# Three dense layers of a transformer stack: norm statistics a turn ahead, second norm on ACT, first norm on POOL in two layers, another order of stages, gate softmax once a layer

## The reference

```
x = x + 0.5 * ffn0(norm(x))      # s = norm @ Win + bin; g = sum_h relu(s*W1+b1)*W2 + b2 (64 channels of 16); g @ Wout + bout
x = x + attention(norm(x))       # 16 heads of 8, 4 kv heads, rotary, causal
x = x + 0.5 * ffn0(norm(x))
x = x + 0.5 * experts(norm(x))   # softmax gate over 8 experts, each takes its top 128 of a sequence's 512 tokens, gelu MLP
x = x + scan(norm(x))            # t = norm @ (sum of U*V + toP); lam = sigmoid(sigmoid(norm @ F) @ W_lam)
                                 # s_t = lam*s_(t-1) + (t @ B); h = (t + s @ C) @ fromP
x = x + 0.5 * experts(norm(x))
```

## Time and profile before

| what | value |
|---|---|
| median of three runs | 1877.16 us (1871.71 to 1878.62) |
| the profiled execution | 1875.22 us, span 1873.2 us |
| mean granted clock of PE | 0.915 |
| busy share: PE, PEld, DVE, ACT, POOL | 84%, 59%, 73%, 58%, 41% |

### The profile page before, as it was taken

The page is one execution under the profiler, slowest core; times in us unless marked ns, Lnnn a source line. Parts: engine busy times, 40 slices in busy tenths (PEclk is TensorE's granted clock), DMA queues, the critical chain, the costliest instruction groups (busy, mean ns, idle before and its releaser), DMA issues. The chain is left out here.

```text
span 1873.2 us, 39185 instructions
## 1 busy us (share of the span) xinstructions
PE 1581.5 (84%) x11698; PEld 1107.9 (59%) x11698; DVE 1360.9 (73%) x3422; ACT 1089.0 (58%) x2225; POOL 760.4 (41%) x1170
## 2 busy tenths in 40 slices
PE   4878749999999999998699529999977751999998
PEld 1444424555555555554355329999964531999997
DVE  4898746777777777774388668777768976777776
ACT  2444313666666666666466427787755531877876
POOL 1565542333333333333233256665401212666540
PEclk9989856999999999999899759999988875999999
DMA  5111231111111111110011301111000110121110
GB/s 135 31 38 50 59 105 36 43 43 42 41 41 41 44 39 42 40 35 2 1 34 33 110 19 39 38 34 29 25 1 23 34 34 12 39 60 46 43 48 23
DMA packets 72819, 76.39 MB, mean 41 GB/s; under 512 B 13040, under 2 KB 61488, under 8 KB 72752
## 3 DMA queue, kind: packets, MB, share of 16 engines
q1 hardware_dynamic: 64560, 58.77, 10.9%
q0 software_dynamic: 8192, 16.79, 3.4%
HBM read 51.40 MB, written 24.12 MB: 40 GB/s over the span
## 5 line engine op out<-in xcount | busy, mean ns | idle before, releaser
L951 DVE TENSOR_REDUCE at_negmax<-at_s_ps 128x2 f32<-128x1024 f32 (+3 forms) x384 | 394.5, 1045 | 174.9 <-PE at_s_ps L741 170.4
L862 ACT ACTIVATE at_p<-at_x_ps 128x512 f32<-128x512 f32 x640 | 353.5, 591 | 224.1 <-PE at_x_ps L751 221.3
L918 POOL TENSOR_SCALAR_AFFINE_SELECT at_p<-at_p 128x256 f32<-128x256 f32 (+1 forms) x448 | 190.7, 438 | 354.9 <-ACT at_p L862 354.9
L1175 POOL DMA_INDIRECT e_x_in<-xn,e_row_c x256 | 258.5, 1010 | 145.7 <-POOL e_row_c L1171 103.5
L739 PE MATMUL at_s_ps<-at_kr,at_qr 72*128 72x512 bf16 (+3 forms) x1024 | 253.0, 312 | 20.6 <-DMA at_kr<-k_parts 18.2
L751 PE MATMUL at_x_ps<-at_qr,at_kr 74*128 74x512 bf16 (+3 forms) x1024 | 236.4, 306 | 23.0 <-ACT at_p L862 12.9
L1296 DVE TENSOR_TENSOR e_hid_lo<-e_hid,e_hid_hi 128x512 fp32r<-128x512 f32 x256 | 177.2, 693 | 85.3 <-ACT e_hid_hi L1260 85.3
L741 PE MATMUL at_s_ps<-maskb,identb 128*128 128x128 bf16 x1024 | 202.1, 225 | 0.0
L1259 ACT ACTIVATE e_hid<-e_h_ps 128x512 f32<-128x512 f32 x256 | 155.0, 605 | 39.4 <-PE e_h_ps L1201 38.9
L766 PE MATMUL at_o_ps<-at_p,at_va 128*32 128x512 f32 (+3 forms) x2048 | 157.0, 449 | 1.6 <-POOL at_p L918 1.6
L1201 PE MATMUL e_h_ps<-e_x_hi,w_hi 128*128 128x256 f32 x512 | 156.0, 305 | 0.1
(11 more groups left out here) (184 smaller groups left out, 3515.2 us busy)
## 6 DMA issues: line engine op xcount, KB each, us to landing
at_qr<-q_parts SPq DMA_DIRECT2D x192, 96.0 KB
k_parts<-m_kparts SPq DMA_DIRECT2D x48, 96.0 KB
at_kr<-k_parts SPq DMA_DIRECT2D x64, 72.0 KB
xres<-in_x_dram SPq DMA_DIRECT2D x8, 512.0 KB, 7.3
xn<-m_n_xhat SPq DMA_DIRECT2D x16, 256.0 KB, 2.3
e_x_in<-xn,e_row_c POOLq DMA_INDIRECT x256, 2.5
xn<-sc_n_xhat SPq DMA_DIRECT2D x16, 256.0 KB, 2.3
out_dram<-xres SPq DMA_DIRECT2D x16, 256.0 KB, 2.3
```

What stands on the lines that cost most here:

```text
L862: a.activation(p_sb[g % 2][:, i, :], x_ps[i % 2][:], ACT.Exp, scale=SCALE).then_inc(x_read, 1)
L918: sel = gp.affine_select(out=part, in_=part, compare_op=ALU.is_ge, fill=0.0, base=0, pattern=[[0, n] for n in part.shape[1:-1]] + [[1, P]] ...
L951: v.tensor_reduce(negmax[u][:, h0:h0 + len(heads), c], s_ps[k % 2][:, 0:len(heads) * pitch].rearrange("p (j w) -> p j w", w=pitch)[:, :, 0:w],
L1175: nc.gpsimd.indirect_dma_start(out=x_in[k][u][:], out_offset=None, in_=xn_dram, in_offset=bass.IndirectOffsetOnAxis(ap=row_c[k][:, u:u + 1 ...
```

## The change

A fourth stage, `ahead`, is put before the head: in each turn DVE makes the first norm's statistics of the next turn (`moments`), and the norm is applied there too, by ACT in the qkv layer and by POOL in the gate and scan layers (`gpsimd_all`). The second norm's statistics are made by DVE in the middle stage, right after the residual is added; ACT applies them (`apply`, an Identity with the root as scale and a shift as bias, which POOL computes), in the mlp layers in the same turn as the statistics, in the scan layer a turn later. For the shift DVE also negates the means (`less`). DVE applies no norm any more.

In the mlp layers DVE's turn is now: statistics ahead, output addition and second statistics of the middle, then (qkv) rotations with hidden channels of the head, or (gate) hidden channels of the head. In the gate layer DVE makes 5 of the 8 channels instead of 3; its scores are made a turn later and its banks of PSUM are shared in another way. POOL's turn begins with the bias addition. The gate's softmax is made once at the end of a layer over all 16 sequences, where the scores of each turn are copied to `probs` (`keep`). In the scan layer `ts` has two buffers. All engines of the scan layer but SP, and the gate layer's POOL, run the turns unrolled (`unrolled`) and not in a loop.

In the scan layer the orders are: PE transposes of the head, products of the middle (L1382, L1383), projection of the head, scores of tail - 1, output of the middle, second transposes of the tail; ACT copies of the head, sigmoid of the middle, second norm of the tail, t and sigmoid of the head, second copies of the tail; POOL root and shift of the tail, then root and application for `ahead`; DVE scans of the middle, statistics ahead, `keep`, output addition and second statistics of the middle. In qkv, PE keeps the order of before.
 `moments`, `statistics` and `aggregate` hold the same instructions as `Norm.moments` before, and `root` the same power as L180. In the diff the lines that begin with "#" only say where what follows stands.

```diff
-HV = {"qkv": 5, "gate": 3}
+HV = {"qkv": 5, "gate": 5}
...
+    def widen(self, dve, i):
...
+        self.nc.vector.tensor_scalar(self.less[:], self.mv[:, :, 0], -1.0, None, ALU.mult)
+        self.nc.vector.tensor_scalar(self.vare[:], self.mv[:, :, 1], EPS, None, ALU.add).then_inc(self.var_done, 1)
...
+    def gpsimd(self, pool, i):
+        self.root(pool, i)
+        self.nc.gpsimd.tensor_tensor(self.shift[:], self.less[:], self.rstd[:], ALU.mult).then_inc(self.shift_done, 1)
...
+    def gpsimd_all(self, pool, i, xhat_used):
+        self.root(pool, i)
+        after(pool, xhat_used, i * W)
...
-                s = self.nc.vector.tensor_scalar(
+                s = self.nc.gpsimd.tensor_scalar(
                     self.xhat[b][:, c * D:(c + 1) * D], self.xres[:, i * W + b, c * D:(c + 1) * D],
                     self.mv[:, j, 0:1], self.rstd[:, j:j + 1], ALU.subtract, ALU.mult)
...
+    def apply(self, act, i):
+        act.wait_ge(self.shift_done, i + 1)
...
+                s = self.nc.scalar.activation(
+                    self.xhat[b][:, c * D:(c + 1) * D], self.xres[:, i * W + b, c * D:(c + 1) * D],
+                    ACT.Identity, bias=self.shift[:, j:j + 1], scale=self.rstd[:, j:j + 1])
...
+def unrolled(turn):
+    at = lambda n: n if 0 <= n < TURNS else None
+    for n in range(TURNS + 3):
+        turn(at(n), at(n - 1), at(n - 2), at(n - 3))
...
 # mlp_layer, PE, gate
+                def turn_gate(ahead, head, middle, tail):
+                    if middle is not None:
+                        channels(middle)
+                    if head is not None:
+                        turn_first(head)
+                    if middle is not None:
+                        output(middle, tail)
+                    if head is not None:
+                        project_in(head)
+                    if tail is not None and not is_first(tail):
+                        score(tail - 1)
+                    if tail is not None:
+                        if middle is not None:
+                            pe.wait_ge(x_added, middle * W + W)
+                        turn_second(tail)
...
 # mlp_layer, ACT, behind the head's channels
+                        split(tail, EARLY[:W])
+                    if not qkv and tail is not None:
+                        copy_second(tail)
+                    if middle is not None:
...
+                        norm2.apply(act, middle)
+                    if qkv and ahead is not None:
+                        norm1.apply(act, ahead)
+                    if qkv and tail is not None:
+                        split(tail, EARLY[W:])
...
 # mlp_layer, POOL, behind the bias addition
+                    if qkv and tail is not None and not is_first(tail):
+                        split(tail - 1, LATE)
+                    if ahead is not None:
+                        if qkv:
+                            norm1.gpsimd(pool, ahead)
+                        else:
+                            norm1.gpsimd_all(pool, ahead, xt_full)
+                    if middle is not None:
+                        norm2.gpsimd(pool, middle)
...
 # mlp_layer, DVE
+                def turn(ahead, head, middle, tail):
+                    if ahead is not None:
...
+                        moments(dve, norm1, ahead)
                     if middle is not None:
...
+                        dve.wait_ge(x_added, middle * W + W)
+                        moments(dve, norm2, middle)
+                    for x in range(NT if qkv else W):
+                        if qkv and tail is not None:
+                            rope(tail, x)
+                        if head is not None and x < W:
+                            hidden(head, x)
...
+                    if not qkv and tail is not None and not is_first(tail):
+                        gate.keep(dve, tail - 1)
...
+                    gate.keep(dve, TURNS - 1)
+                    gate.softmax(dve)
```

More of the change, by code:

```diff
@@ new lines, in project_in, with score, turn_qkv @@
+                def project_in(head):
+                    for b in range(W):
+                        pe.wait_ge(xt_read, head * W + b + 1)
+                        pe.matmul(s_ps[b][:], h["win2"][:], xhat_t[b][:], start=True, stop=True).then_inc(s_full, 1)
+                def score(tail):
+                    pe.wait_ge(xt2_read, tail * W + W)
+                    for b in range(W):
+                        gate.tensor(pe, tail, b, xhat2_t[b])
+                def turn_qkv(ahead, head, middle, tail):
@@ L436, in turn @@
                     if tail is not None:
-                        if qkv:
-                            queries(tail, 1)
-                            keys(tail)
-                            values(tail)
-                        else:
-                            for b in range(W):
-                                gate.tensor(pe, tail, b, xhat2_t[b])
-                pipeline(pe, turn)
+                        queries(tail, 1)
+                        keys(tail)
+                        values(tail)
@@ L447, in _ @@
+                pipeline(pe, turn_qkv if qkv else turn_gate)
+                if not qkv:
+                    score(TURNS - 1)
             @block.scalar
@@ L461, in split @@
                             a.activation(r["parts"][:, 1, :], r["b"][:], ACT.Copy).then_inc(p2_done, 1)
-                def turn(head, middle, tail):
-                    if not qkv and tail is not None and not is_first(tail):
-                        gate.scalar(act, tail - 1)
+                def turn(ahead, head, middle, tail):
                     if middle is not None:
@@ L1374, in _, with turn @@
             def _(pe):
-                def turn(head, middle, tail):
+                def turn(ahead, head, middle, tail):
+                    if head is not None:
+                        for b in range(W):
+                            pe.wait_ge(norm1.xhat_done, head * W + b + 1)
+                            if tail is not None and not is_first(tail):
+                                pe.wait_ge(xt2_read, tail * W - W + b + 1)
+                            transpose_chunks(pe, xt_ps[b], norm1.xhat[b], h["ident"]).then_inc(xt_full, 1)
                     if middle is not None:
@@ L1414, in _, with turn @@
                 a = nc.scalar
-                def turn(head, middle, tail):
-                    if tail is not None and not is_first(tail):
-                        gate.scalar(act, tail - 1)
+                def turn(ahead, head, middle, tail):
+                    if head is not None:
+                        for b in range(W):
+                            act.wait_ge(xt_full, head * W + b + 1)
+                            a.activation(xhat_t[b][:], xt_ps[b][:], ACT.Copy).then_inc(xt_read, 1)
                     if middle is not None:
@@ L1451, in _, with turn @@
                 v = nc.vector
-                def turn(head, middle, tail):
-                    if tail is not None:
-                        dve.wait_ge(x_added, tail * W + W)
-                        norm2.moments(dve, tail)
-                        if not is_first(tail):
-                            gate.less_max(dve, tail - 1)
-                    if head is not None:
-                        norm1.moments(dve, head)
-                    if tail is not None:
-                        for b in range(W):
-                            after(dve, xn_out[b], tail * 16)
-                        norm2.apply(dve, tail)
+                def turn(ahead, head, middle, tail):
                     if middle is not None:
```

286 lines of the change are left out of this document (136 added, 150 removed).

## The result

| | before | after |
|---|---|---|
| median of four runs, us | 1875.68 (1871.71 to 1878.62) | 1885.85 (1882.14 to 1887.94) |
| span of the profiled run, us | 1873.2 | 1880.1 |
| mean granted clock | 0.915 | 0.915 |

The account below looks back on a forecast made before the run. DVE was taken to bound qkv and scan, while PE in gate had about 1 us idle a turn. 1875.2 - 26 (qkv) + 15 (gate) - 15 (scan) = 1849.2, about 1850 on the median's footing; range 1832 to 1864.

Parts of the forecast that it names:

- qkv, -26: qkv layer: 26 us shorter, from five turns won 20, start lost 3, end won 10, 1 off; range -38 to -10.
- gate, +15: Gate layer: 15 us longer, 12 from seven turns, 1.5 at the start, 1.5 in the tail.
- the collision: Gate layer: POOL's bias adds, 2.5 us, stretch DVE's hidden channels 5 to 8, adding 1.7 us a turn.
- The ring without collision at 16.5: Gate turn: sum read, output, adds, second moments, DVE's hidden channels, channel sums; 16.5 us, equal to before.
- scan, -15: Scan layer: 122 us against 137.1, a turn 12.1 for 15.4; bounds -22 and -8.
- with pointers I take 0.35, so 2.8 us a norm: POOL's norm: 8 tensor_scalar of 128x128 at 0.35 us each; bounds 0.2 and 1.65 each.
- a ring that took its PE work at warm durations: Scan turn: scans, moments ahead, root, POOL's norm, transposes, lambda product, sigmoid, next scan; 12.1 us a turn.
- about 15 ... as before: Scan layer start: about 15 us after the layer's first instruction, unchanged from before.
- The tail of the scan layer, 25: Scan layer after the last scan: 25 us for output, moments, norm, cold scores and softmax 4.3.
- D: Rival: POOL's tensor_scalar priced like its power, 1.65 us each; 1924, spread over 1860 to 1924; chance 0.14.
- B: Rival: no collision in the gate layer, gate +3, rest as forecast, 1838 (1828 with dense PE in qkv); chance 0.16.
- C: Rival: ACT's queue takes DVE's place in qkv, turn stays at 27, gate and scan as forecast, 1875; chance 0.10.

## Why the prediction was wrong

- **qkv, -26: right, also by its terms.** -28.3 in the profile of after, 24.0 to 27.4 in the twelve others. The five turns win 21.9 us (forecast 20), the start loses 3.8 (3), the end wins 10.2 (10). The turn is 23.5 for the forecast 23.3; ACT's Identity lasts 0.48 one by one, but eight take 3.19 us (forecast 3.2), PE's clock 0.88 before and 1.00 after. DVE also waits there for ACT's application before it may aggregate, 22.6 us in sum, which I had not seen; since the turn came out at its forecast length, I take it to be off the path, which no run tested. The upper bound of 6.4 for eight applications was worked out wrongly: a 512-column one takes 0.71 by its own row, so 5.7. Nothing hung on it.
- **gate, +15: sign right, 5.5 too much, and both by luck.** Of the 15, 12 were to come from the collision and 1.5 from the start; of the measured 9.5, the steady turns gave 0.4, the first turns 7.6 and the tail 1.5 as forecast. "channels 5 to 8 ... 1.7 us: 18.2 a turn" failed. The ring without collision at 16.5 was right (16.6, and the order of the ten channels moves it to 14.92). I had POOL free at 8.6 us; its norm takes 6.6 us and not 2.8, so root and shift end at 10.4, and the bias addition meets the last two channels. The slow POOL took the collision off the path: with a norm of 4.8 us it was on it (17.3). The start took 5.0 more than before (forecast 1.5), where POOL's norm stands with 6.2 for DVE's 2.1, and the next turn 2.6 more, 1.5 of it cold channel sums (8.59 for 7.08).
- **scan, -15: wrong, +27.9; this is the failed step, "with pointers I take 0.35, so 2.8 us a norm".** The row that it was nearest to gave columns (0.9 ns each), and I put almost nothing beside them. The size was off by 0.44 us on each of eight instructions, 6.2 us a norm for 2.8. In the turn: 12.1 + 3.4 = 15.5, and 16.0 was measured at full clock. The cold clock adds 1.5: 17.5. That term was missing altogether, in a ring that took its PE work at warm durations although has 0.83 in this very stretch.
- **The start of the scan layer, "about 15 ... as before":** the first scan came 24.95 us after the layer's first instruction, before 14.0. Two POOL norms stand in a row (timeline of after):

```profile
1384.19 6.23 POOL L205 TENSOR_SCALAR sc_n_xhat<-xres,sc_n_mv,sc_n_rstd 128x128 f32<-128x128 f32 x8 [0.31 <-POOL sc_n_rstd L189]
...
1390.59 0.64 DVE L176 BATCH_NORM_AGGREGATE sc_n_mv<-sc_n_stats 128x2 f32<-128x6 f32 x8 [7.34 <-POOL sc_n_xhat L205]
...
1393.79 6.22 POOL L205 TENSOR_SCALAR sc_n_xhat<-xres,sc_n_mv,sc_n_rstd 128x128 f32<-128x128 f32 x8 [0.31 <-POOL sc_n_rstd L189]
...
1400.06 1.12 PE L279 MATMUL sc_xt_ps<-pack,sc_n_xhat 128*128 128x128 f32 x4 [2.44 <-POOL sc_n_xhat L205]
1401.11 1.11 PE L1459 MATMUL sc_tf_ps<-sc_fg,wlam 64*64 64x512 f32 x1
```

  PE's order puts the next turn's transposes (1400.06) ahead of this turn's lambda products (1401.11), so the first scan waits for the second norm too. With ACT's norm the first scan still came 22.2 us after the start; with DVE's, 16.0.
- **The tail of the scan layer, 25:** 25.2 as forecast, before 19.7. The single softmax costs the tail what the forecast said, 4.1 us: five operations of 0.55 to 0.69 us behind the last scores.
- **The sum of the scan layer:** 122 was forecast. The best form measured, with norm by ACT and warm clock, is 22.2 to the first scan + 90.2 of scans + 24.7 = 137.2, no better than the 138.2 of before. So even then the new form (statistics ahead, norms on ACT, one softmax, idle matmuls; no run takes them apart) gives 2 us a turn and takes them back at both ends: 8 at the start, 5 in the tail.
- **Rivals.** D, "decides from about 0.85 us each", is the one that came true in kind, at 0.79, below its own point: it counted only seven turns of 8 x 0.44, not start and clock. B's gate turn of 16.5 came too (16.6), but not its gain: the gate layer gave +9.5 for its +3. C did not come: the qkv turn is 23.5 and not 27. The chance of 0.13 for slower was too low for a new operation whose price stood in no row.

## What to carry to other kernels

An operation whose price no row shows decides the forecast when a ring goes through it: work the sum out at its upper bound before giving the sign a chance, and count it at the layer's start as well. Where an engine waits in each turn, take PE's work behind the wait at the cold durations of that stretch. Where a consumer alternates between two sequences, the producer should too: that order alone was worth 10 us of the gate layer here where POOL's bias addition missed the channels, and 6 where it held one up.

## What was not expected of the hardware

- POOL's tensor_scalar on 128x128 f32 takes 0.60 us (one operation, one pointer), 0.64 (two operations, constants), 0.79 (two operations, two pointers), where an affine select of 128x256 took 0.41. The Trainium skill, page "GPSIMD Engine Reference", section "3.1 Elementwise — side-by-side cycle accounting", has 769 ns for 512 elements in a tight loop, its best case; 128 columns took as long here, 0.79 us. Only this width was run, so no run here tells how much of it goes by columns.
- Idle matmuls alone brought PE's clock from 0.79 to 1.00 in the scan layer and shortened the turn by 1.5 us, and in the form with ACT's norm from 0.84 to 1.00, and the turn from 14.8 to 13.05.
- A hidden channel on DVE that comes up beside a POOL tensor_tensor is held until that is over (1.49 us for 0.54), one channel for each POOL instruction, not all stretched in proportion. The five channels of the earlier trace rows show it already: by the view of the tile three of them take 0.53 us and two 1.49 and 1.51, one for each of the two POOL instructions.
